# A graph network's edge loop: gathering 64-wide node rows instead of 128-wide products

## The reference

```python
h = relu(layernorm(x)); msg_in = concat([h[src], edge_attr_9, edge_attr_8])      # 64 + 9 + 8
m = silu(silu(msg_in @ W1 + b1) @ W2 + b2) @ W3 + b3                             # 81 -> 128 -> 128 -> 64
agg = segment_sum(m, dst)
upd = concat([h, agg])
gate = sigmoid(upd @ G + gb)
u = silu(layernorm(upd @ U1 + ub1) * ln1_g + ln1_b)
out = x + h + gate * (layernorm(u @ U2 + ub2) * ln2_g + ln2_b)
```

## Time and profile before

| what | us |
|---|---|
| median of three runs | 3270.5 |
| lowest and highest | 3262.56, 3275.14 |
| span of the profiled execution | 3264.2 |
| TensorE busy | 2847.1 (87%) |
| GpSimd busy | 1565.9 (48%) |
| ScalarE busy | 1543.7 (47%) |
| VectorE busy | 1468.1 (45%) |

### The profile page before, as it was taken

How to read it: one execution, slowest core, us unless ns; L and a number is a source line. 1 busy time by engine, 2 the same in 40 slices (tenths; PEclk the granted TensorE clock), 3 DMA queues, 4 the chain that set the end, 5 groups by cost and what they waited for, 6 DMA issues and landing times.

```text
span 3264.2 us, 59125 instructions
## 1 busy us (share of the span) xinstructions
PE 2847.1 (87%) x18211; PEld 2118.1 (65%) x18211; DVE 1468.1 (45%) x2016; ACT 1543.7 (47%) x2600; POOL 1565.9 (48%) x1663
## 2 busy tenths in 40 slices
PE   3599999859999969899989888988888989998894
PEld 2477777759989955566555555555555655655563
DVE  7999999863445543222222222222222222222227
ACT  2588888723332214444444444444444444444456
POOL 4000000000000017777777777777777777777765
PEclk8799999959999979999999999999999999999995
DMA  3133333429979966776776777777676777767752
GB/s 127 62 155 157 143 152 157 168 79 370 364 314 352 347 196 181 189 195 189 191 192 189 189 189 194 189 194 189 190 193 189 191 189 190 195 191 191 192 155 68
DMA packets 355148, 632.41 MB, mean 194 GB/s; under 512 B 42566, under 2 KB 251017, under 8 KB 336092
## 3 DMA queue, kind: packets, MB, share of 16 engines
q1 hardware_dynamic: 299973, 519.99, 48.1%
q0 software_dynamic: 54128, 110.18, 15.0%
q10 hardware_dynamic: 1001, 1.66, 0.1%
HBM read 391.13 MB, written 240.52 MB: 194 GB/s over the span
## 4 chain that ended last, share of the span: by engine, by line
PE 37%; POOL 29%; issue 12%; DMA 12%; DVE 8%; ACT 1%; POOLq 0%; DVEq 0%; ACTq 0%
POOL arena L635 27%; PE ps L772 17%; DMA arena<-p_tab,m_idx 11%; PE ps L791 6%; PE ps L949 5%; PE ps L968 3%; DVE arena L1807 2%; PE ps L958 2%; PE ps L946 2%; DVE stageT L1783 2%; POOL arena L648 1%; PE ps L673 1%; PE ps L823 1%; PE ps L661 1%; POOL arena L576 0%
## 5 line engine op out<-in xcount | busy, mean ns | idle before, releaser
L635 POOL DMA_INDIRECT arena<-p_tab,m_idx x1563 | 1474.7, 944 | 1611.2 <-issue 1568.5
L2029 DVE TENSOR_TENSOR_SCAN arena<-arena,ps 128x512 f32<-128x512 f32 x391 | 500.4, 1280 | 1033.8 <-ACT ps L1280 1019.7
L949 PEld LDWEIGHTS ps<-ident,arena 128*128 128x128 f32 x3126 | 391.6, 197 | 517.6 <-DMA arena<-p_tab,m_idx 426.6
L968 PEld LDWEIGHTS ps<-w_fold,arena 128*128 128x128 f32 x3128 | 555.1, 198 | 202.8 <-issue 202.8
L1275 ACT ACTIVATE arena<-ps 128x512 f32<-128x512 f32 x391 | 233.5, 597 | 887.1 <-PE ps L949 884.1
L949 PE MATMUL ps<-ident,arena 128*128 128x128 f32 x3126 | 468.7, 295 | 203.0 <-DMA arena<-p_tab,m_idx 201.7
L968 PE MATMUL ps<-w_fold,arena 128*128 128x192 f32 x3128 | 593.7, 335 | 0.0
L772 PE MATMUL ps<-arena 128*128 128x195 bf16 (+1 forms) x4802 | 481.1, 248 | 31.9 <-DVE arena L1749 31.3
L772 PEld LDWEIGHTS ps<-arena 128*128 128x128 f16 x4802 | 416.5, 98 | 62.8 <-DVE arena L1749 31.5
L946 PE MATMUL ps<-arena,weights 17*128 17x512 f32 x782 | 440.9, 643 | 1.7 <-issue 1.7
L958 PE MATMUL ps<-arena,weights 128*128 128x512 f32 x782 | 427.5, 630 | 0.0
(11 more groups left out here) (257 smaller groups left out, 1637.8 us busy)
## 6 DMA issues: line engine op xcount, KB each, us to landing
arena<-count_d SPq DMA_DIRECT2D x98, 1568.0 KB, 8.6
scan_rows<-arena SPq DMA_DIRECT2D x391, 384.0 KB, 3.5
arena<-keep_d SPq DMA_DIRECT2D x391, 256.0 KB, 4.6
count_d<-arena SPq DMA_DIRECT2D x49, 1568.0 KB, 5.1
arena<-p_tab,m_idx POOLq DMA_INDIRECT x1563
arena<-attr_in SPq DMA_DIRECT2D x391, 34.0 KB
p_tab<-ends SPq DMA_DIRECT2D x12, 256.0 KB, 5.0
wide<-hT_d SPq DMA_DIRECT2D x1, 1617.0 KB
```

The lines of the kernel that those rows point to most:

```text
L635: pool.indirect_dma_start(m_rows[:, k, t, :], None, p_tab, bass.IndirectOffsetOnAxis(ap=m_idx[:, k, t:t + 1].bitcast(U32), axis=0))\
L949: last = pe.matmul(x[:, t * P:(t + 1) * P], m_rows[:, k, t, :], ident[:, :], start=False, stop=(t == tiles_of - 1), skip_group_check=True)
L968: last = pe.matmul(m_back[h][:, t * ROW:(t + 1) * ROW], m_scan[:, k % SCAN_RING, e_at:e_at + P], w_fold[:, :], start=True, stop=True)
L2029: dve.tensor_tensor_scan(m_scan[:, k % SCAN_RING, :], m_mask[:, k, :], m_term[k % TERM_RING], before, ALU.mult, ALU.add).then_inc(e1.scan_ ...
```

## The change

The table holds the normalised rows themselves, 64 numbers (`m_tab`), so the table product and its bias add go away. In the loop TensorE turns four gathered tiles into one bank (`turn_rows`), VectorE copies them into the upper 64 rows of a tile whose other 17 hold the attributes (`keep_turned`), and one product with all 81 rows of W1 follows a slot later (`hidden_in`); b1 comes in with ScalarE's silu. W2 stands two slots behind the turn, the scan three, the product back four; that product is with W3 alone, 64 columns. So `scan_rows` has 64 numbers per edge, stored in runs of 1 KB, for which the index of the last edge is rearranged in eight more small steps. Laps are of twelve slots, the ring of gathered rows has twelve, that of masks six. The multiplication with the lower half of the update weights moves from the loop to the end stage: for each group the fetched rows are turned (`turn_agg`), copied by ScalarE (`copy_agg`) and multiplied (`agg_product`), and VectorE adds from PSUM. The groups are nine, of six or fewer tiles.

```diff
-LOOP = 8
+LOOP = 12
-ROW_RING = MASK_RING = LOOP
-ATTR_RING, TERM_RING, SCAN_RING, OUT_RING = 4, 4, 4, 4
-LAG = 3
+ROW_RING = LOOP
+MASK_RING = 6
+ATTR_RING, TERM_RING, SCAN_RING, OUT_RING = 4, 3, 4, 4
+HID_RING, BACK_RING = 2, 1
+LAG, SCAN_LAG = 4, 3
-END_GROUPS = [(0, 7), (7, 7), (14, 7), (21, 7), (28, 7), (35, 7), (42, 4), (46, 3)]
-GATES_AT = {1: (0, 2), 3: (2, 4), 5: (4, 6), 7: (6, 8)}
+END_GROUPS = [(0, 6), (6, 6), (12, 6), (18, 6), (24, 6), (30, 6), (36, 6), (42, 4), (46, 3)]
+GATES_AT = {1: (0, 2), 3: (2, 4), 5: (4, 6), 7: (6, 8), 8: (8, 9)}
...
-                    pool.indirect_dma_start(m_rows[:, k, t, :], None, p_tab,
+                    pool.indirect_dma_start(m_rows[:, k, t, :], None, m_tab,
...
-            def hidden_in(s, k, lap, tiles_of=TB):
-
-                x = m_in[k % 2]
+            def turn_rows(s, k, lap, tiles_of=TB):
+
+                pe.wait_ge(e1.gathered[k], DMA * (TB * lap + tiles_of))
+                if not isinstance(lap, int) or s >= 1:
+                    pe.wait_ge(e1.turn_kept, s)
+                pe.sem_inc(alone, 1)
+                for t in range(TB):
+                    last = pe.transpose(m_turn[:, t * P:(t + 1) * P], m_rows[:, k, t, :], ident[:, :])
+                last.then_inc(e1.turn_done, 1)
+
+            def hidden_in(s, k, lap):
+
                 pe.wait_ge(e1.attr_loaded[k % ATTR_RING], DMA * ((LOOP // ATTR_RING) * lap + k // ATTR_RING + 1))
-                if not isinstance(lap, int) or s >= 2:
-                    pe.wait_ge(e1.silu1_done, s - 1)
-                pe.matmul(x, W("W1e"), m_attr[:, k % ATTR_RING, :], start=True, stop=False, skip_group_check=True)
-                pe.wait_ge(e1.gathered[k], DMA * (TB * lap + tiles_of))
-                for t in range(tiles_of):
-                    last = pe.matmul(x[:, t * P:(t + 1) * P], m_rows[:, k, t, :], ident[:, :],
-                                     start=False, stop=(t == tiles_of - 1), skip_group_check=True)
-                last.then_inc(e1.in_done, 1)
+                pe.wait_ge(e1.turn_kept, s + 1)
+                if not isinstance(lap, int) or s >= 1:
+                    pe.wait_ge(e1.silu1_done, s)
+                pe.matmul(m_in, W("W1"), m_msg[:, k % ATTR_RING, :], start=True, stop=True).then_inc(e1.in_done, 1)
...
+            def turn_agg(i, a, n):
+
+                pe.wait_ge(rows_fetched[i], n * DMA)
+                if i >= 1:
+                    pe.wait_ge(agg_copied, i)
+                else:
+                    pe.wait_ge(h_kept, KEEP_UNITS)
+                for t in range(n):
+                    last = pe.transpose(ps[0:D, 3 + t // TB, (t % TB) * P:(t % TB + 1) * P], ybuf[:, a + t, :], ident[:, :])
+                last.then_inc(agg_turned, 1)
...
             for i, (a, n) in enumerate(END_GROUPS):
-                turn_update(i, n)
-                update_out(i, n)
+                turn_agg(i, a, n)
+                agg_product(i, n)
+                if i >= 1:
+                    turn_update(i - 1, END_GROUPS[i - 1][1])
+                    update_out(i - 1, END_GROUPS[i - 1][1])
...
+            def copy_agg(i, n):
+
+                act.wait_ge(agg_turned, i + 1)
+                if i >= 2:
+                    act.wait_ge(agg_multiplied, i - 1)
+                act.activation(aggT[:, i % 2, 0:n * P], ps[0:D, 3:5, :].rearrange("p b c -> p (b c)")[:, 0:n * P], ACT.Copy)\
+                   .then_inc(agg_copied, 1)
...
             for i, (a, n) in enumerate(END_GROUPS):
+                copy_agg(i, n)
+                if i >= 1:
+                    hidden_update(i - 1, END_GROUPS[i - 1][1])
                 square_u(i, a, n)
                 roots(i, i, i - 2 if i >= 2 else None)
                 if i >= 1:
                     square_v(i - 1, *END_GROUPS[i - 1])
-                hidden_update(i, n)
                 if i in GATES_AT:
                     gates(*GATES_AT[i])
...
+            def keep_turned(s, k):
+
+                dve.wait_ge(e1.turn_done, s + 1 + ROW_RING)
+                if not isinstance(s, int) or s >= ATTR_RING:
+                    dve.wait_ge(e1.in_done, s - ATTR_RING + 1)
+                dve.tensor_copy(m_msg[0:D, k % ATTR_RING, :], m_turn).then_inc(e1.turn_kept, 1)
```

More of the change, by code:

```diff
@@ L443, in by_edges @@
                 first_slots()
-                with sp.Fori(0, NG) as g:
-                    sp.wait_ge(node_used, G_TABLE + g + 3)
-                    sp.dma_start(p_rows[:, bass.ds(g * GT, GT), :], wide[:, bass.ds(g * GT, GT), :]).then_inc(p_stored, DMA)
-                load_hT(NG)
+                sp.wait_ge(table_rows, 1)
+                sp.dma_start(tab_rows, hbuf[:, :, :]).then_inc(m_stored, DMA)
+                load_hT(1, NG)
             def by_counts():
@@ L761, in by_edges @@
                     layer_product(l)
-                node_phase(G_TABLE, D, [(W("W1x"), HID)], turned=D + 2)
-                pe.wait_ge(node_used, G_TABLE + NG + 2)
-                pe.sem_inc(node_turned, G_AFTER - G_TABLE - NG)
-                pe.sem_inc(node_product, G_AFTER - G_TABLE - NG)
+                pe.wait_ge(node_used, G_TABLE + 2)
+                for g in range(NG):
+                    turn(G_TABLE + g, g % 2, D + 2)
             def by_counts():
@@ L834, in turn_table @@
                     last.then_inc(table_turned, 1)
-                def multiply_table(k):
-                    pe.wait_ge(table_copied, k + 1)
-                    if not isinstance(k, int) or k > 0:
-                        pe.wait_ge(table_used, k)
-                    for t in range(tiles(k)[1]):
-                        last = pe.matmul(ps[:, 6, t * HID:(t + 1) * HID], stageT[0:D, 1, t * P:(t + 1) * P], W("W1x"),
-                                         start=True, stop=True)
-                    last.then_inc(table_product, 1)
                 def body(l, k, begun=0):
@@ L919, in by_counts @@
                         body(l, 1)
-                        turn_w3()
                     else:
@@ L1003, in h_product, with agg_product @@
                 last.then_inc(h_multiplied, 1)
+            def turn_agg(i, a, n):
[7 more added lines that the diff above has]
+                last.then_inc(agg_turned, 1)
+            def agg_product(i, n):
+                pe.wait_ge(agg_copied, i + 1)
+                if i >= 1:
+                    pe.wait_ge(u_ready, i)
+                for t in range(n):
+                    last = pe.matmul(ps[:, t // 2, (t % 2) * ROW:(t % 2 + 1) * ROW], aggT[:, i % 2, t * P:(t + 1) * P], W("UGa"),
+                                     start=True, stop=True)
+                last.then_inc(agg_multiplied, 1)
             def turn_update(i, n):
@@ L1367, in _ @@
             last = len(END_GROUPS) - 1
+            hidden_update(last, END_GROUPS[last][1])
             roots(last + 1, None, last - 1)
@@ L1931, in body @@
                     use_tiles(l, k - 1)
-                    if l == LAYERS - 1 and not (isinstance(k, int) and k == 1):
-                        use_table(k - 2)
                     stage_tiles(link, l, k)
@@ L2050, in add_h @@
-                dve.wait_ge(h_kept, (a + n - 1) // 4 + 1)
-                rows_of = of_rows[:, a:a + n, :]
-                dve.tensor_tensor(rows_of, rows_of, of_h[:, a:a + n, :], ALU.add).then_inc(u_ready, 1)
+                dve.wait_ge(agg_multiplied, i + 1)
+                even = n - n % 2
+                last = dve.tensor_tensor(of_rows[:, a:a + even, :].rearrange("p (b t) f -> p b (t f)", t=2), ps[:, 0:even // 2, 0:2 * ROW],
+                                         of_h[:, a:a + even, :].rearrange("p (b t) f -> p b (t f)", t=2), ALU.add)
@@ L2054, in add_bias @@
+                if n > even:
+                    last = dve.tensor_tensor(of_rows[:, a + even, :], ps[:, even // 2, 0:ROW], of_h[:, a + even, :], ALU.add)
+                last.then_inc(u_ready, 1)
             def add_bias(i, a, n):
                 dve.wait_ge(v_done, i + 1)
-                dve.tensor_tensor(ybuf[:, a:a + n, :], ps[:, 6, 0:n * D].rearrange("p (t c) -> p t c", c=D),
+                dve.tensor_tensor(ybuf[:, a:a + n, :], ps[:, 7, 0:n * D].rearrange("p (t c) -> p t c", c=D),
@@ L2155 @@
     rowsv = {"b_in": a[g0 + "b_in"], "b_l": a[g0 + "b_l"], "gamma": a[g0 + "gamma_l"], "beta": a[g0 + "beta_l"]}
-    rowsv.update({n: a[g1 + n] for n in ("b1", "ub2", "ln2_g", "ln2_b")})
+    rowsv.update({n: a[g1 + n] for n in ("ub2", "ln2_g", "ln2_b")})
     v = np.concatenate([rowsv[n].reshape(-1) for n in V_COLS]).reshape(1, V_TOTAL)
```

252 lines of the change are left out of this document (128 added, 124 removed).

## The result

The changed kernel took 3321.6 us (median of four runs, 3310.3 to 3331.8), the kernel before 3272.8 us on the same chip: ratio 1.015, 95% interval 1.0112 to 1.0188. The forecast was 3294.9 us and slower. The time lies inside the stated range (3272 to 3345) and outside the likeliest case's own (3283 to 3306).

What follows compares the result with a forecast made beforehand. GpSimd's row gathers were taken to bound 1951 us, 60% of the span. Terms 0 - 10.1 - 5.0 + 1.9 + 1.0 + 36.6 = +24.4 us, added to the 3270.5 us median, gave 3294.9 us; range 3272 to 3345.

Steps and rivals of the forecast that it cites:

- likeliest case: Whole kernel: the forecast itself, 3294.9 us, slower, with its own range 3283 to 3306; chance 0.60.
- largest term: End stage: turn, copy and product added per group make a closed round at half clock, +38.0 us, +36.6 after credit.
- rival (d): Edge loop: VectorE's copy of the turned rows holds GpSimd, +49 us, 3344 us in all; chance 0.05.
- The bound of the loop: Edge loop: GpSimd's 1563 gather issues at 1.248 us stay 1951 us, change 0.
- (c): Edge loop: TensorE stays at the half clock, +512 us, 3807 us in all; chance 0.11.
- (e): Edge loop: shorter rows issue faster, 2% of 1951 us or -39, 3256 us in all; chance 0.04.
- Ahead of the loop: Before the loop: table product gone -10.1 us, store after last staging earlier -5.0, index arithmetic +1.9.
- lose it under the sums: Table stage: nine full bodies lose the 1.09 us table product each, one single-tile body 0.3, together -10.1 us.
- clock credit: End stage: 1.4 us less because the clock is still high for the first turn.
- Rival (a): End stage: runs at full clock, +17.5 us instead of +36.6, 3275.8 us in all; chance 0.16.
- Rival (b): End stage: its added work hides altogether behind GpSimd's 49 gathers, 3258.3 us in all; chance 0.04.
- The term for the drain: Draining the loop: one more copy and W2-like step, shorter copy out and store, +1.0 us (0 to +5 if clock low).

Runs made afterwards that it cites:

- e13_fold: Changed kernel with the 192-column product back (W3 folded with the update weights) and end stage of the kernel before: 3261.5 against 3270.1 us, ratio 0.9973.
- e5_warm: Changed kernel plus unused 256-column products after the last four products back and 512-column ones in the end stage: ratio 1.0032 to the kernel before.
- e11_before: The kernel before, unchanged, traced again on a chip where every kernel took some 700 us longer; no total time given.
- before: First profiled execution of the kernel before, unchanged: span 3264.2 us.
- e7_after: The changed kernel, unaltered, run again on a chip where every kernel took some 700 us longer: ratio 1.0087 to the kernel before.
- after: First profiled execution of the changed kernel: span 3330.0 us.

## Why the prediction was right, and what it missed

- **In short.** The direction and the mechanism of the largest term were right, the size was half: +48.8 us between the medians, +24.4 forecast. That the time still lies inside the range is in part luck: the range reached up to 3345 us for the sake of rival (d), which did not come, and 3321.6 lies in that part of it. No error cancelled another: every term came out slower than forecast.
- **The bound of the loop.** Right: 1563 issues at 1.25 us, no wait. TensorE's clock from 1300 to 3100 us sank from 0.97 to 0.84, and to 0.90 with the wider product back (`e13_fold`), and the backlog always went. Rivals (c), (d) and (e) fall: no stuck clock, no held gather (946 ns, and the same with twice the copies), and 256-byte rows are not issued faster than 512-byte ones (946 against 944 ns).
- **Ahead of the loop.** Right in kind, a third too large (-9.8 measured, -13.2 forecast; the index arithmetic cost its 1.9). A body takes 18.33 instead of 19.10 us (turns L811 at 1141.06 and 1159.39; before, L815 at 1056.01 and 1075.11): the product's 1.09 went, but the turn now meets VectorE:

```profile
1159.39 0.60 PE L811 MATMUL ps<-ident,stage 128*128 128x128 f32 x4
1160.22 0.60 PE L829 MATMUL ps<-ident,stage 128*66 128x128 f32 x4 [0.23 <-DVE stage L1946]
```

  The step that failed is "lose it under the sums": the bodies had no gap, and I gave the freed time to nobody. Behind the last staging 3.5 instead of 5.0 us were saved; from the end of the relu to the first gather it is 4.8 us, from the end of the bias add before 3.9.
- **The end.** The term rested on a round worked out step by step at the half clock, and it hit: adds within 0.3 us, the stretch 119.4 instead of 118.0 (116.6 with the clock credit). Rival (a) did not come by itself; `e5_warm` shows that its round of 7 to 9.7 us exists (7.7) if TensorE is given wide products. Rival (b) falls. The row that I held against rival (a), 20 us at 0.50 from 665 us on the earlier trace rows, is not a fixed property of that code: in `e11_before`, the same kernel, the same products came to the full clock after some 5 us. 14 records in `before`, then in `e11_before`:

```profile
664.41 3.09 PE L673 MATMUL ps<-weights,stageT 128*128 128x64 f32 x14
```

```profile
685.66 1.67 PE L673 MATMUL ps<-weights,stageT 128*128 128x64 f32 x14
```

  So this row could decide neither (a) nor (c).
- **The missing term.** "The first turn also waits for all of h, kept at 3182.17": I took that time from before and moved nothing ahead of it but 1.0 us of drain. Before, 24 records of 192 columns ran up to the product of h without a pause, and it kept the full clock. The change made these narrow, and pauses opened between them; I counted that as less work, with a clock credit of 1.4 us on top. It cost 15.3 us. The term for the drain was too small as well, 3.4 us instead of 1.0; the pauses are not the whole reason, since `e13_fold`, without them, needs 3.8.

The Trainium skill (TensorE: Matmul & The Clock Gate, HAM oscillation) says that bursts of matmuls parted by waits are run at the half clock over and over. I weighed it for the loop, where it costs nothing. The trace agrees in kind at the place where I didn't apply it: behind pauses of 0.56 us the product of h took 31.67 instead of 16.09 us.

Of the 41.4 us between the forecast span (3288.6) and the measured one, 15.3 are the product of h, 13.7 the start, 3.9 the gathers' pace, 3.4 the table stage, 2.4 the drain and 2.7 the end. The start is the first node products at half clock in that execution: 3.25 us for 14 records against 1.80 (the clock column reads 1.00 there in both, so the durations have to be read). It is no part of the change: before's own code had them at half clock in `e11_before`, and in `e7_after` they began at full clock. Without it 52.0 us are left between the spans, close to the 48.8 between the medians.

The changed kernel's times fall into two pairs (3310 and 3332), and the traces show two places where one and the same code differs from execution to execution: the start, 13.8 us, and the stretch from the index arithmetic to the last staging of h, 532.7 us in `after` and 523.8 in `e7_after` (before 539.0, in `e11_before` 531.8), where the clock came back early or not, as in the rows above. Together they are 22.7 us, the pairs are 21 apart. That it is these two stays unproven: only one execution of the four was traced. The saving ahead of the loop was forecast from rows of one execution, too.

## What to carry to other kernels

Making a matmul narrower isn't only less work: on a path where it covered waits it opens pauses, and what follows can pay with a halved clock (15.3 us here). So price each stage behind a thinned one at both clock levels. Work moved out of a loop in which TensorE has slack to a serial tail lands on the path with its whole length, copy, turn and waits included. Before a clock in one trace is taken for a property of the code, look at a second execution. And in such a tail issue the next group's turn and copy ahead of this group's product: 18.5 us here for moving the turn on TensorE and the copy on ScalarE.

## What the runs showed of the hardware

- The half clock can outlast full business: in `after` the 98 records of the product of h ran 31.67 us without a pause at 0.50, while the same records, begun at 1.00, ran 16.09 us at 1.00 in `before` and `e13_fold`. In `e5_warm` it rose in the rows where 512-column products stood.
- The same code can meet either level: the products from 657 us on stayed at 0.50 in `before` (14 records in 3.09 us) and rose after some 5 us in `e11_before` (1.67).
- An indirect DMA of 128 rows costs GpSimd 0.94 to 0.95 us and 0.30 to the next for rows of 256, 512 and 768 bytes alike. In the end stage before, ten of 49 were stretched (1.25 to 1.83 us) where VectorE added and scaled from SBUF. In `after` the adds read PSUM and the scalings stand further apart: one of 49 was stretched (1.41 us), and they went out in 60.5 us instead of 65.1.
- On three of the chips the edge loop of every kernel stops 126 to 154 times for some 2 to 12 us, several engines at once, in part with releasers that stand as "remote" in the profile; the start and the stretch behind the loop are stopped as well. The cause is not known.
